# One adaLN block on one core: new order of the prologue, and of x1, P and h2 inside a step

## The reference

```python
h = _layernorm(x, axis=-1) * (1 + ca) + sa
x = x + ga * _L0_attn_ref(h, L0_attn_Wq, L0_attn_Wk, L0_attn_Wv, L0_attn_Wo)
h = _layernorm(x, axis=-1) * (1 + cb) + sb
x = x + gb * _L0_ffn_ref(h, L0_ffn_factors, L0_ffn_bias)
```

## Time and profile before

| | us |
|---|---|
| median of 3 runs | 455.6 |
| lowest, highest | 452.86, 457.02 |
| the profiled execution | 454.29 |
| its span, first to last instruction | 452.5 |

### The profile page before, as it was taken

The page is one execution under the profiler, slowest core; times in us unless marked ns, Lnnn a source line. Parts: engine busy times, 40 slices in busy tenths (PEclk is TensorE's granted clock), DMA queues, the critical chain, the costliest instruction groups (busy, mean ns, idle before and its releaser), DMA issues. The chain is left out here.

```text
span 452.5 us, 7294 instructions
## 1 busy us (share of the span) xinstructions
PE 441.0 (97%) x2118; PEld 363.6 (80%) x2118; DVE 356.4 (79%) x610; ACT 319.6 (71%) x642; POOL 233.1 (52%) x308
## 2 busy tenths in 40 slices
PE   8999996999999999999999999999999999999996
PEld 7686885888888888888888888887788888887885
DVE  5677654587887978988877978896887877999977
ACT  3676663677978676888868787876878564667761
POOL 1528337262555635466555645465555427168882
PEclk9999998999999999999999999999999999999999
DMA  8999997123477356778596366767687136758423
GB/s 324 391 407 312 218 191 112 48 81 106 141 240 225 116 188 191 250 193 251 168 255 206 116 190 218 233 189 203 181 245 219 48 121 201 215 163 280 128 83 139
DMA packets 77750, 88.05 MB, mean 195 GB/s; under 512 B 5000, under 2 KB 55944, under 8 KB 77200
## 3 DMA queue, kind: packets, MB, share of 16 engines
q1 hardware_dynamic: 73872, 80.51, 57.0%
q0 software_dynamic: 3264, 6.29, 8.0%
q10 hardware_dynamic: 576, 0.79, 0.5%
HBM read 53.49 MB, written 34.10 MB: 194 GB/s over the span
## 5 line engine op out<-in xcount | busy, mean ns | idle before, releaser
L1667 POOL TENSOR_SCALAR ve<-mv 128x1 f32<-128x1 f32 x64 | 21.1, 330 | 164.1 <-DVE mv L1304 115.2
L525 PE MATMUL ps_o<-v_hi,pt_lo 128*128 128x512 f32 x192 | 74.7, 389 | 0.0
L524 PE MATMUL ps_o<-v_lo,pt_hi 128*128 128x512 f32 x192 | 74.7, 389 | 0.0
L526 PE MATMUL ps_o<-v_hi,pt_hi 128*128 128x512 f32 x192 | 74.7, 389 | 0.0
L860 ACT ACTIVATE h_f<-x1b,mod_t 128x128 f32<-128x128 f32 x120 | 53.1, 598 | 5.5 <-DVE x1b L1322 5.3
L1189 DVE TENSOR_TENSOR h_lo<-h_f,h_hi 128x512 fp32r<-128x512 f32 x57 | 42.8, 750 | 8.9 <-ACT h_hi L832 8.6
L524 PE MATMUL ps_v<-wvo_lo,h_hi 128*128 128x512 f32 x112 | 45.5, 406 | 1.1 <-DVE h_lo L1189 1.1
L908 ACT ACTIVATE probs<-ps_s,negmax 128x1024 f32<-128x1024 f32 x32 | 35.4, 1108 | 12.7 <-DVE negmax L1248 12.1
L525 PE MATMUL ps_v<-wvo_hi,h_lo 128*128 128x512 f32 x112 | 44.3, 396 | 0.0
L526 PE MATMUL ps_v<-wvo_hi,h_hi 128*128 128x512 f32 x112 | 44.2, 394 | 0.0
L1669 POOL TENSOR_TENSOR rstd<-ve,minus_half 128x1 f32<-128x1 f32 x64 | 41.3, 646 | 5.3
(11 more groups left out here) (232 smaller groups left out, 1179.2 us busy)
## 6 DMA issues: line engine op xcount, KB each, us to landing
x_blocks<-xn SPq DMA_DIRECT2D x50, 256.0 KB, 2.7
p_blocks<-probs SPq DMA_DIRECT2D x24, 512.0 KB, 3.5
pb<-p_blocks SPq DMA_DIRECT2D x96, 128.0 KB, 3.1
x1b<-x_blocks SPq DMA_DIRECT2D x30, 256.0 KB, 2.9
result<-x_ring SPq DMA_DIRECT2D x15, 512.0 KB, 3.0
xb<-x_blocks SPq DMA_DIRECT2D x20, 256.0 KB, 2.9
x_ring<-in_x SPq DMA_DIRECT2D x18, 256.0 KB, 3.2
wmod<-in_wmod SPq DMA_DIRECT2D x4, 1024.0 KB, 15.4
```

Source lines behind the costliest of these rows:

```text
L524: nc.tensor.matmul(acc, a_hi, b_lo, start=first, stop=False)
L525: nc.tensor.matmul(acc, a_lo, b_hi, start=False, stop=False)
L526: return nc.tensor.matmul(acc, a_hi, b_hi, start=False, stop=last)
L1667: nc.gpsimd.tensor_scalar(ve[:, one], mv[:, u, 1:2], EPS, None, ALU.add).then_inc(ve_done, 1)
```

## The change

No instruction is added or taken away; only their order changes, and the waits with it.

In a step, SP sends x1's blocks (`send_x1`) ahead of `fetch_p`, and x's blocks (`send_x`) ahead of `send_p`. ACT norms x1 first, then modulates the turned x1, and rounds h2 right behind it. DVE takes the rest of the values ahead of turning x, and the rest of h2 ahead of turning P. In the prologue the calls of ACT, DVE and POOL are reordered; on POOL the first accumulating DMAs go out behind `of_x(3)`, and `of_x(TB + 2)`, the constants of tile 10, comes ahead of four of them. The diff, less the hunk of ACT's prologue:

```diff
@@ -454,18 +454,18 @@
                     fetch_x(t + TB + 1, 1 - u)
                 if opening is not None:
                     send_p(opening)
+                if 1 <= t < T - 1:
+                    send_x1(t - 1, 1 - u)
                 if t + 1 < T and not turned_by_pe(t + 1):
                     fetch_p(t + 1)
-                if 1 <= t < T - 1:
-                    send_x1(t - 1, 1 - u)
                 if u and g >= 2:
                     store_pair(g - 2)
                 if 1 <= t < T - 1:
                     fetch_x1(t - 1, 1 - u)
+                if 12 <= t + TB + 2 < T:
+                    send_x(t + TB + 2, u)
                 if scored_in(t) is not None and not turned_by_pe(scored_in(t)):
                     send_p(scored_in(t))
-                if 12 <= t + TB + 2 < T:
-                    send_x(t + TB + 2, u)
                 if t < T - TB and t % TB in (2, 4):
                     spread_gate(t % TB // 2 - 1, t // TB + 1)
                 if 2 * TB <= t + TB + 3 < T and t >= 5:
@@ -927,6 +927,7 @@
                 act.wait_ge(nmr2_done, t + 1)
                 if isinstance(t, int) and t < 2:
                     act.wait_ge(xt_ps, TB + 3 + t)
+                    wait(act, x2n_out, 16 * t)
                 elif after_x:
                     act.wait_ge(xn_out, 16 * (t - 1))
                 else:
@@ -1003,10 +1004,11 @@
                 probs_part(t, 1)
                 if parts is not None:
                     parts(1)
+                if t:
+                    normalize_x1(t - 1, 1 - u, q < T)
                 if t >= 2:
                     modulate_x1(t - 2, batch_of((t - 2) // 2))
-                if t:
-                    normalize_x1(t - 1, 1 - u, q < T)
+                    h2_upper(t - 2)
                 if q < T and q not in late_x_banks:
                     modulate_x_turned(q, batch_of(q // 2))
                 if q < T:
@@ -1017,8 +1019,6 @@
                     exponentials(scored_in(t))
                 if behind is not None:
                     behind()
-                if t >= 2:
-                    h2_upper(t - 2)
                 if q + 1 < T:
                     if q + 1 in late_x_banks:
                         normalize_x(q + 1, u)
@@ -1086,28 +1086,28 @@
             values_of(1)
             h_of(3)
             x_row(4)
+            values_of(2)
             h_of(4)
-            qk(1)
-            values_of(2)
             x_row(5)
             x_row(6)
+            qk(1)
             h_of(5)
-            h_of(6)
+            x_row(7)
             values_of(3)
             values_of(4)
-            x_row(7)
+            h_of(6)
+            qk(2)
             copy_rows()
-            qk(2)
+            pair_q(0)
             x_row(8)
+            values_of(5)
             h_of(7)
-            values_of(5)
+            h_of(8)
             values_of(6)
-            h_of(8)
-            pair_q(0)
             qk(3)
             values_of(7)
+            normalize_x(TB + 1, 1)
             exponentials(0)
-            normalize_x(TB + 1, 1)
             step(0)
             step(1)
             act.wait_ge(mod_t_done, 4)
@@ -1346,9 +1346,9 @@
                 probs_rest(t, 1)
                 if t == 2:
                     turn_x1(0)
+                values(t + TB)
                 if q < T and q not in late_x_banks:
                     turn_x(q)
-                values(t + TB)
                 if scored_in(t) is not None:
                     row_max(scored_in(t))
                 if q + 1 < T:
@@ -1362,10 +1362,10 @@
                     x_moments(q + 1, u)
                 if q < T:
                     h_rest(q, 1 - u)
+                if t >= 2:
+                    h2_rest(t - 2)
                 if not turned_by_pe(t + 1):
                     turn_p(t + 1)
-                if t >= 2:
-                    h2_rest(t - 2)
                 if ahead_of_gate is not None:
                     ahead_of_gate()
                 if t < T - TB - 1:
@@ -1520,36 +1520,36 @@
             h_first(2)
             h_second(2)
             qk(0)
+            pair_q(0)
             h_first(3)
             h_second(3)
+            moments_of(6)
             values_of(1)
-            moments_of(6)
+            moments_of(7)
+            values_of(2)
             h_first(4)
+            h_second(4)
             qk(1)
-            h_second(4)
-            values_of(2)
             h_first(5)
             h_second(5)
-            moments_of(7)
+            values_of(3)
             moments_of(8)
             moments_of(9)
-            values_of(3)
+            values_of(4)
             h_first(6)
             h_second(6)
-            values_of(4)
             bound_gates()
             h_first(7)
             h_second(7)
             qk(2)
-            pair_q(0)
             values_of(5)
+            h_first(8)
             values_of(6)
-            h_first(8)
             h_second(8)
             qk(3)
             row_max(0)
+            other_columns()
             values_of(7)
-            other_columns()
             step(0)
             dve.wait_ge(bias_loaded, 16)
             step(1)
@@ -1763,29 +1763,29 @@
                 add_half(i, 1)
 
             last_wv_rest()
+            wqk_rest()
             of_x(2, 0)
-            wqk_rest()
             of_x(3, 1)
+            add_factor(1)
             of_x(4, 0)
             of_x(5, 1)
             of_x(6, 0)
-            add_factor(1)
+            of_x(7, 1)
+            add_factor(2)
             add_factor(5)
-            of_x(7, 1)
             of_x(TB, 0)
             of_x(TB + 1, 1)
-            add_factor(2)
+            add_factor(6)
+            of_x(TB + 2, 0)
+            add_factor(7)
             add_factor(3)
-            add_factor(6)
-            add_factor(7)
-            of_x(TB + 2, 0)
             of_x1(0, 0)
+            of_x(TB + 3, 1)
             sum_factors(0)
             sum_factors(1)
             sum_factors(2)
-            of_x(TB + 3, 1)
+            sum_factors(3)
             of_x1(1, 1)
-            sum_factors(3)
             pool.wait_ge(bias_loaded, 16)
             for k in range(C):
                 pool.wait_ge(f_hi_done, k + 1)
```

More of the change, by code:

```diff
@@ L1068, in _ @@
             nc.scalar.activation(silu_den[:], c_sb[:], ACT.Exp, scale=-1.0).then_inc(silu_exp, 1)
+            wv_upper(2)
             wo_upper(2)
-            wv_upper(2)
             x_row(0)
```

## The result

| | before | changed |
|---|---|---|
| median of 17 runs, us | 455.0 | 457.6 |
| lowest, highest | 452.56, 457.02 | 456.68, 460.49 |
| the profiled execution | 454.29 | 457.12 |
| its span | 452.5 | 455.3 |

The changed kernel takes 1.0066 times as long as before (95% interval 1.0046 to 1.0085): 0.7% or 2.7 us slower, where -0.2 us was predicted (455.4 against 455.6). The time lies inside the range given, but on the other side of before. The 17 runs put before at 455.0, where the prediction had 455.6 from three.

What follows compares the result with a forecast made beforehand. PE was taken to bound the kernel, busy 441.0 of 452.5 us. Prologue -4.3 and steps +4.8 gave +0.5 on the profiled 454.3, so 454.8; median forecast 455.4, own range 452.5 to 458, with rivals 450 to 460.5.

Steps and rivals of the forecast that it cites:

- the other moves: Prologue: remaining reorderings sit in idle time of ACT and DVE; taken at 0, otherwise 0.3 to 0.7 us.
- the early accumulation: Prologue: first accumulating DMAs go out some 10 us earlier, beside loads of x; range 0 to 0.7 us, taken at 0.
- the ring: Steps: loop nmr, norm, P's fetch and turning, gate, nmr; 26.0 us per two steps against PE's 25.0 and 24.1.
- followed from step 8: Steps 8 to 15: loop on time at step 11, 1.0 us late at 13, 2.6 at 15; 2.5 us a batch.
- The hole at 70 us: Prologue: PE's wait for tile 10's normed x and the low clock after it go; -5.7 us, bounds -5.7 and 0.
- The sum of the factors is next: Prologue: the last four DMAs delay x1(1)'s constants, so PE waits for step 2's exponentials; +1.4 us, bounds 0 and 2.5.
- third rival: Prologue: early accumulation delays loads of x, PE waits about 4 us at 33.9 us; about 460 us, chance 0.04.
- fourth rival: Prologue: POOL's wait stays as an earlier DMA lands after 69, 5.7 us not gained; about 460 us, chance 0.04.
- The first part, nmr to h_lo of 6.2 us: Steps 7, 15, 23: ACT's work behind nmr makes h_lo late; PE waits 0.9, 1.2 and 1.2 us.
- gain nothing: Steps: h2's earlier rounding and rest, and values ahead of turning x, gain nothing; PE waited only 0.5 us for these.
- Sending x ahead of P: Steps, on SP: holds P back by 2 us or so, still landing well before its fetch; cost 0.

Runs made afterwards that it cites:

- e5: Before with the changed kernel's new prologue and, of the steps, only ACT's norm of x1 first: 452.2 us, 0.9930 of before.
- e9: e5 with ACT's early rounding of h2 (right behind the modulation of x1) added: 458.5 us, 1.0067 of before.
- e4: The changed kernel with P fetched ahead of sending x1 on SP, as before: 464.9 us, 1.0219 of before.
- e10: e5 with SP sending x1 ahead of fetching P added: 455.2 us, 1.0021 of before.
- e11: e5 with SP sending x ahead of sending P added: 461.5 us, 1.0120 of before.
- S1: The change's move on SP that sends x1 ahead of fetching P; added to e5 it gave 455.2 us.

## Why the prediction was wrong, step by step

The steps that failed are two sizes in the sum, each 1.1 us too low in cost: in the prologue, what stands at 0 for the other moves and the early accumulation, and in the steps, the ring "followed from step 8". The sum itself said +0.5 us; that the forecast reads -0.2 comes from laying 454.8 to 456.1 beside a median of three runs, 455.6, which was 0.6 high.

- **The hole at 70 us**: right, 5.3 us gained where 5.7 were predicted. The constants were ready at 70.59 rather than 69.5, since the moments came a microsecond later (as PE itself was late by that) and the three instructions took 1.70 us, not 1.34.
- **The sum of the factors is next**: right. Last landing 84.5 (predicted 83), constants at 88.56 (87.5), 1.2 us back (1.4). Before's own wait there was 0.23 us and not the 0.4 of the prediction, which leaves its 1.4 as it is.
- **"The other moves of the prologue ... taken at 0"**: mis-sized. PE waits 0.8 us for `qk_lo` at 53.3 and loses 0.97 us in all; the bound of 0.7 given for it was too small. It is no move of ACT or DVE that comes late, as the prediction allowed for (DVE's calls around this `qk_lo` stand in the same order as before), but POOL: the constants of tile 8 now stand behind the DMAs of factors 2 and 5. POOL can issue the second DMA of factor 2 only when that of factor 1 has landed, at 41.15, and the first of factor 5 only when the load of factor 4 has, at 44.34. The constants are ready at 48.94 where it was 44.58. ACT idles 2.09 us for them, and the norm, h of tile 7 and the rest `qk_lo` follow one another. The load of factor 4, before and changed (tile wmod, the DMA issued at 16.65), and constants and norm of tile 8 in the changed kernel; the last row is those constants in before:

```profile
DMA to landing us min/median/max: 21.1/21.1/21.1
```

```profile
DMA to landing us min/median/max: 27.7/27.7/27.7
```

```profile
44.63 2.42 POOL L1743 DMA_DIRECT2D wmod<-in_factors  x2 [1.99 <-DMA wmod<-in_factors]
...
48.68 0.26 POOL L1671 TENSOR_SCALAR nmr<-mv,rstd 128x1 f32<-128x1 f32 x1 [0.21 <-POOL rstd L1669]
...
48.97 0.81 ACT L1052 ACTIVATE xn<-x_ring,nmr,rstd 128x512 f32<-128x512 f32 x1 [2.09 <-POOL nmr L1671]
```

```profile
44.32 0.26 POOL L1671 TENSOR_SCALAR nmr<-mv,rstd 128x1 f32<-128x1 f32 x1 [0.57 <-ACT probs L1052]
```

This chain is read from the traces; no run puts the constants of tile 8 ahead alone. Prologue: -3.2 measured, -4.3 predicted. This is half of the miss.
- **Early accumulation holds up x** (third rival): no hole at 34 us, and pair 3 landed at 31.3 as before. But the mechanism is there, on the loads behind it: pair 4 landed at 38.85 instead of 35.11, factor 4 at 44.34 instead of 37.81, pair 5 at 48.14 instead of 39.12, though all were issued at the same times as before. Factor 4's is a link of the chain above. POOL's wait stays (fourth rival): no.
- **The first part, nmr to h_lo of 6.2 us, waits at steps 7, 15, 23**: right in the changed kernel (nmr to h_lo 6.2 us; 0.8 us at step 7; 1.3 idle at 15 and 23), but put on the wrong move. I charged it to the norm's coming first; e5 shows that it costs nothing until h2's rounding joins it (e9), the very edit of which I wrote that it can "gain nothing", without asking what stands behind it.
- **The ring**: right in place and length, 25.85 us for two steps against 26.0 predicted. I had it as a matter of fetching P; e4, e9 and e10 show two arms, through P's landing and through ACT, each sufficient. That the length came out is partly luck: in step 10 P landed at nmr + 6.05, not 6.9, and it was ACT's rounding and DVE's two rests, done at nmr + 6.8, that turning P stood behind.
- **"Followed from step 8, it is on time at step 11"**: wrong, and the other half of the miss (0.5 us of idle time at step 11, and 0.2 ahead of it in step 10). The steps took 3.7 us in the second batch where I had 2.5. Step 9 was counted with the 8.05 us read in step 14, an even step. It took 9.6 us, from nmr at 178.32 to the gate at 187.92:

```profile
177.91 0.41 POOL L1671 TENSOR_SCALAR nmr<-mv,rstd 128x1 f32<-128x1 f32 x1 [0.21 <-POOL rstd L1669]
178.28 1.29 POOL L1684 TENSOR_TENSOR ffn<-ffn,bias_bc 128x512 f32<-128x512 f32 x1
...
181.45 1.52 POOL L1701 TENSOR_TENSOR x_ring<-ffn,x_ring 128x512 f32<-128x512 f32 x1 [0.18 <-POOL ffn L1690]
...
178.30 3.52 DVE L1189 TENSOR_TENSOR pt_lo<-pb,pt_hi 128x512 fp32r<-128x512 f32 x2
181.75 0.68 DVE L1189 TENSOR_TENSOR v_lo<-ps_v,v_hi 128x512 fp32r<-128x512 f32 x1
182.35 0.69 DVE L1318 STREAM_TRANSPOSE xb<-xb 128x512 f32<-128x512 f32 x1
...
187.92 0.71 DVE L1287 SCALAR_TENSOR_TENSOR attn<-ps_o,rden,gates 128x512 f32<-128x512 f32 x1
...
183.08 1.39 ACT L860 ACTIVATE h_f<-xb,mod_t 128x128 f32<-128x128 f32 x3 [1.43 <-DVE xb L1318]
```

Two rests `pt_lo` took 3.52 us together, where one takes 0.67 (mean of the 26 from P's trip that no 128x512 instruction of POOL overlaps), because POOL's bias, gate and sum ran beside them; then came the values, and only then xb, which had landed at 179.33 and for which ACT waited until 183.08. Before had the same slow pair in step 9, but xb was turned next, and the gate of step 8 came 0.1 us behind PE's last matmul, where in the changed kernel it came 0.75 behind. Even in before, step 9 took 9.0 us from nmr to gate, so that 8.05 was too short for it in any order. In the third batch, where step 17 took 8.2 us, the predicted 1.4 us were measured.
- **Sending x ahead of P**: priced at 0 in the prediction, and the worst move of all by itself (e11). In the changed kernel S1 hides most of it.

Sum: -3.2 and +5.9 where -4.3 and +4.8 stood, both 1.1 us off to the same side. The forecast of no change rested on two terms of opposite sign, and the direction on less than either's error: with terms of 4 to 5 us each and bounds of some 2 us, the sum could not tell faster from slower.

## What to carry to other kernels

Where a wait is moved to the front of an in-order queue, write the whole loop out (here nmr, norm, both modulations, roundings, rest, turning, gate, nmr) and compare it with what the bounding engine needs. In e5 two steps of the loop take about PE's 25.0 us and the move is free; with 0.8 us more in the even step (e9) they take 25.7 and more, and the kernel loses 6.3 us, of which the loop's own waits are a good half. Measure the loop in every kind of step, odd and even, and not in one: the odd ones are bound by other work of the same engine. A move priced at nothing because nobody waits for what it brings early must still be priced for what it now stands in front of: that was so of the rounding of h2, of x's blocks, and of the accumulating DMAs ahead of tile 8's constants. And where transfers are started earlier, look at all the loads that are still under way, and not at the nearest alone.

## What the runs showed of the hardware

- DVE's `pt_lo` and `h_lo`, which read two operands of SBUF, and POOL's 128x512 work hold each other up: `pt_lo` took 1.8 us each in step 9, where POOL had begun first, and 0.67 without it. In step 11 `pt_lo` began 0.1 us ahead of POOL's L1684: it took 0.68, and POOL's took 1.75 instead of 1.29. `v_lo`, one of whose operands is in PSUM, took 0.65 to 0.69 beside the same POOL instructions, and `negmax` and `stats` did not slow, either. This agrees with the Trainium skill, "SBUF — State Buffer", section "Who interferes with whom": an instruction of DVE with two SBUF inputs contends with one of GpSimd that reads SBUF, and the later of the two waits.
- xb's 256 KB landed 4.0 us after issue in step 11 of e5, and 6.5 us in e11, where the 512 KB of P had gone out 2.5 us ahead of it; in step 12 of e11, with P 2.0 us ahead and no load of the gates, 3.0 us. Which resource they share was not tried.
- With POOL's accumulating DMAs started at 26.5 instead of 36.1 us, loads that SP had issued at 16.0 to 19.9 us, and that were due from 35 us on, landed 3.7 to 9.0 us later; the one due at 31.2 did not move.
